# Tokens of a selective scan by VectorE block transpositions and SBUF-to-SBUF transfers in place of TensorE transposes

## The reference

```python
zxbcdt = x @ Win                       # per direction; 256 -> 512 (z) + 640 (x, B, C) + 8 (dt)
xBC = silu(causal_conv4(xBC) + convb)  # depthwise, 4 taps
dt = softplus(dt + dtb); dA = exp(dt * A)
h = dA_t * h + dt_t * B_t (x) x_t      # per head: 8 heads of 64, state 64; scan over 512 tokens
y = C_t . h + D * x
y = y * silu(z); y = y * rsqrt(mean(y*y) + 1e-5) * normw
out = y @ Wout                         # reversed direction likewise, on flipped tokens
x = x + concat(out_fwd, out_rev) @ Wo + bo
x = x + layernorm(x) @ W.T + b + (layernorm(x) @ V_r) @ C.T
```

## Time and profile before

| | |
|---|---|
| median of 3 runs | 630.82 us (629.98 to 631.05) |
| span of the profiled execution | 629.0 us |
| TensorE busy | 592.0 us, 94% |
| ScalarE busy | 547.2 us, 87% |
| VectorE busy | 503.6 us, 80% |
| POOL busy | 409.4 us, 65% |
| granted TensorE clock, mean | 0.995 |

### The profile page before, as it was taken

One profiled execution on the slowest core, in us unless ns is written; L12 is line 12 of the kernel. 1 busy time (PEld: TensorE's weight loads), 2 busy tenths in 40 slices (PEclk: granted clock), 3 DMA queues, 4 the chain that ended last, 5 costly groups with the idle time before them and its releaser, 6 DMA issues.

```text
span 629.0 us, 13895 instructions
## 1 busy us (share of the span) xinstructions
PE 592.0 (94%) x4320; PEld 461.0 (73%) x4320; DVE 503.6 (80%) x991; ACT 547.2 (87%) x1197; POOL 409.4 (65%) x427
## 2 busy tenths in 40 slices
PE   1998999999999999999999999999999999999995
PEld 1776687777877777777877778777777777777784
DVE  2669788996979879797888969798797978879663
ACT  4689998979999899988999799897999989997952
POOL 1006948787486864878476874868648684768843
PEclk9999999999999999999999999999999999999997
DMA  7533514236061541418132360614416170343500
GB/s 220 189 109 115 198 40 124 92 106 203 8 200 27 171 114 41 169 28 255 28 116 95 107 204 0 211 25 160 126 28 182 26 241 12 92 122 99 181 1 33
DMA packets 43545, 70.71 MB, mean 112 GB/s; under 512 B 8000, under 2 KB 30592, under 8 KB 43520
## 3 DMA queue, kind: packets, MB, share of 16 engines
q1 hardware_dynamic: 43520, 70.40, 36.7%
HBM read 59.37 MB, written 4.72 MB: 102 GB/s over the span
## 4 chain that ended last, share of the span: by engine, by line
PE 55%; ACT 18%; DVE 13%; issue 8%; POOL 3%; SPq 1%; DMA 1%; DVEq 0%; ACTq 0%; POOLq 0%
PE mi L621 14%; ACT bs L968 8%; PE pj L487 7%; PE py L580 7%; PE pj L489 6%; PE pj L488 6%; DVE xc L1378 5%; PE mi L687 4%; PE py L598 3%; ACT bs L974 2%; ACT L953 2%; DVE bs L1405 2%; DVE ss L1437 2%; ACT xc L935 1%; DVE xres L1445 1%
## 5 line engine op out<-in xcount | busy, mean ns | idle before, releaser
L1378 DVE SCALAR_TENSOR_TENSOR xc<-pj,cw,xc 128x510 f32<-128x510 f32 (+2 forms) x240 | 175.4, 744 | 24.9 <-ACT xc L935 23.0
L968 ACT ACTIVATE bs<-bs,s_all 128x128 f32<-128x128 f32 x512 | 158.4, 388 | 0.2
L1892 POOL TENSOR_TENSOR yg<-yg,sz 128x512 f32<-128x512 f32 x60 | 76.9, 1287 | 81.6 <-DVE yg L1424 81.6
L487 PE MATMUL pj<-xnt_hi,w_hi 128*128 128x512 f32 x288 | 126.1, 438 | 0.9 <-DVE xc L1378 0.8
L489 PE MATMUL pj<-xnt_hi,w_lo 128*128 128x512 f32 x288 | 114.2, 396 | 0.0
L488 PE MATMUL pj<-xnt_lo,w_hi 128*128 128x512 f32 x288 | 113.8, 395 | 0.0
L621 PE MATMUL mi<-wc,yg 128*128 128x256 f32 x480 | 112.1, 386 | 0.8 <-DVE xres L1445 0.2
L621 PEld LDWEIGHTS mi<-wc,yg 128*128 128x128 f32 x480 | 88.6, 190 | 16.9 <-issue 3.3
L1405 DVE TENSOR_TENSOR bs<-bs,gm 128x512 f32<-128x512 f32 x128 | 86.1, 680 | 8.5 <-ACT bs L974 7.7
L1871 POOL TENSOR_TENSOR xw<-xdt,w_end 128x512 f32<-128x512 f32 x48 | 49.6, 1045 | 49.8 <-ACT w_end L953 40.9
L1390 DVE TENSOR_TENSOR xdt<-mi,dt 128x512 f32<-128x512 f32 x64 | 42.8, 688 | 44.6 <-PE mi L547 44.2
(11 more groups left out here) (149 smaller groups left out, 1021.6 us busy)
## 6 DMA issues: line engine op xcount, KB each, us to landing
bs<-rows_dram SPq DMA_DIRECT2D x64, 512.0 KB, 5.4
es<-rows_dram SPq DMA_DIRECT2D x128, 96.0 KB, 3.0
xres<-in_x SPq DMA_DIRECT2D x8, 512.0 KB, 3.6
cc<-bcm SPq DMA_DIRECT2D x32, 128.0 KB, 2.3
out<-ot SPq DMA_DIRECT2D x32, 128.0 KB, 3.4
xin<-in_x SPq DMA_DIRECT2D x7, 512.0 KB, 5.3
rows_dram<-s_rows SPq DMA_DIRECT2D x128, 4.0 KB
cz<-bcm SPq DMA_DIRECT2D x16, 128.0 KB, 2.4
```

Source lines behind the costliest of these rows:

```text
L487: pe.matmul(ps[:], hi(k), xnt_hi[:, k, :], start=(k == 0), stop=False)
L968: i = nc.scalar.activation(bs[:, h, Q * c:Q * c + Q], bs[:, h, Q * c:Q * c + Q], ACT.Relu, bias=s_all[:, d, 0, c, h:h + 1], scale=-1.0)
L1378: i = dve.scalar_tensor_tensor(xc[:, t, to], pj[bank][:, of], cw[:, d, t, KW - 1 - s:KW - s], xc[:, t, to], ALU.mult, ALU.add)
L1892: pool.tensor_tensor(yg[:, d, p, :], yg[:, d, p, :], sz[:, d, p, :], ALU.mult).then_inc(yg_ready, 1)
```

## The change

TensorE transposes neither x nor B any more. `turn` (VectorE) transposes each of the five tiles of a unit, four of `xs` and the one of `bcm`, in blocks of 32x32. Its output goes into `turned`, in which the five tiles lie interleaved: one tile's elements are five words (20 bytes) apart. This puts the tokens in the right order within each block of 32 partitions. `carry` (SP) then moves the blocks to their partitions, with 16 SBUF-to-SBUF transfers per unit, each from 32 partitions to 32 partitions in runs of 640 bytes (80 KB), into `tok`. `step` (VectorE) multiplies the x part of `tok` with dt in place, four times per unit. `state` and `intra` read their weights, and `decayed_x` its input, from `tok`, at every fifth word. `xw` now lies in the same bytes as `turned`. The copies of B (ScalarE) and 5 of the 19 uses of the `mi` banks per unit go. `decayed_c` now waits for C's copies itself. All engines' lists of calls, and SP's, are put in new orders, the opening's loads too.

```diff
+SQ = 32
+BLK = P // SQ
...
-        xdt = sb("xdt", [P, NC, DI])
-        xw = sb("xw", [P, NC - 1, DI])
-        btok = sb("btok", [P, NC, NS])
+        turned = sb("turned", [P, BLK, NC, SQ * (1 + KI)])
+        xw = turned[:].rearrange("p b c r -> p (b c r)")[:, 0:(NC - 1) * DI].rearrange("p (j n) -> p j n", j=NC - 1)
+        tok = sb("tok", [P, NC, P, 1 + KI])
...
+            def carry(b, d):
+                sp.wait_ge(turn_ready, (1 + KI) * (2 * b + d + 1))
+                alone(sp)
+                pair_done(b, d, KI - 1)
+                for i in range(BLK):
+                    for q in range(BLK):
+                        sp.dma_start(tok[SQ * q:SQ * q + SQ, :, SQ * i:SQ * i + SQ, :].rearrange("p c r t -> p c (r t)"),
+                                     turned[SQ * i:SQ * i + SQ, q]).then_inc(tok_loaded[i], 16)
...
-            def b_tokens(phase, it, b, d):
...
-            def x_tokens(phase, it, b, d, j):
...
-                                   btok[:, ORDER[d][j], :], heads[:, :, MEMBERS[half], :], start=True, stop=True, skip_group_check=True)
+                                   tok[:, ORDER[d][j], 0:NS, KI], heads[:, :, MEMBERS[half], :], start=True, stop=True, skip_group_check=True)
...
+                if p == 0:
+                    pe.wait_ge(step_ready, NC * (u + 1))
...
-                        pe.matmul(py[bank][HP * half:HP * half + HP, Q * c:Q * c + Q], xdt[:, c, HP * h:HP * h + HP],
+                        pe.matmul(py[bank][HP * half:HP * half + HP, Q * c:Q * c + Q], tok[:, c, HP * half:HP * half + HP, p],
...
+            def turn(b, d, t):
+
+                u = 2 * b + d
+                if t < KI:
+                    dve.wait_ge(xs_ready, KI * u + t + 1)
+                else:
+                    dve.wait_ge(bc_ready, u + 1)
+                dve.transpose(turned[:].rearrange("p b c (r t) -> p c b r t", t=1 + KI)[:, :, :, :, t],
+                              xs[:, d, t, :] if t < KI else bcm[:, d, :]).then_inc(turn_ready, 1)
+
+            def step(b, d, j):
+
+                if j == 0:
+                    for i in range(BLK):
+                        dve.wait_ge(tok_loaded[i], 16 * BLK * (2 * b + d + 1))
+                    dve.wait_ge(dt_ready[d], b + 1)
                 c = ORDER[d][j]
...
+                own = tok[:, c, :, 0:KI].rearrange("p (z q) t -> p z t q", z=2)
+                i = dve.tensor_tensor(own, own, dt[:, d, c, :].rearrange("p (t z) -> p z t", z=2).unsqueeze(3).broadcast_to([P, 2, KI, HP]),
+                                        ALU.mult)
+                i.then_inc(step_ready, 1)
...
+                pool.wait_ge(step_ready, NC * (2 * b + d) + j + 1)
...
+                if p == 0:
+                    pool.wait_ge(cc_loaded[d], 48 * (b + 1))
```

More of the change, by code:

```diff
@@ L1556, in reversed_scan @@
+                outputs(b, 1, 1)
+                weights(phase, it, b, 1, 7)
+                conv(nxt, 0, 2, 3)
                 conv(nxt, 0, 4, 1)
+                turn(nxt, 0, 4)
+                conv(nxt, 0, 3, 3)
                 conv(nxt, 0, 4, 2)
-                conv(nxt, 0, 3, 3)
+                turn(nxt, 0, 0)
                 conv(nxt, 0, 4, 3)
+                turn(nxt, 0, 1)
+                turn(nxt, 0, 2)
+                turn(nxt, 0, 3)
+                s_rest(phase, it, 0)
                 outputs(b, 1, 2)
@@ L1612, in first_scan @@
+                turn(b, 1, 4)
+                weights(phase, it, b, 0, 7)
+                turn(b, 1, 0)
+                turn(b, 1, 1)
+                s_rest(phase, it, 1)
+                turn(b, 1, 2)
+                turn(b, 1, 3)
                 outputs(b, 0, 2)
@@ L1710, in forward_scan @@
-                conv(b, 1, 1, 3)
-                norm2_bn(phase, it, last, 1)
+                turn(b, 1, 4)
+                s_copy(phase, it, 1)
+                conv(b, 1, 2, 2)
+                norm2_aggr(last, 0)
+                norm2_aggr(last, 1)
+                outputs(b, 0, 0)
+                conv(b, 1, 2, 3)
+                weights(phase, it, b, 0, 5)
                 mix(phase, it, last, 1, 2)
```

762 lines of the change are left out of this document (358 added, 404 removed).

## The result

The changed kernel takes 753.64 us (751.9 to 756.03) beside 630.4 us (629.89 to 631.05) for the kernel before on the same chip: 1.196 times the time, interval 1.193 to 1.199. I had forecast 680 us and a range of 617 to 730. The direction was right; the measured time lies outside the range, 74 us above the forecast. The profiled execution spans 752.0 us, 123.0 more than the 629.0 before.

The account below looks back on a forecast made before the run. TensorE, busy 72.0 of 73.6 us a turn, bounds the kernel; the change moves the bound to VectorE. Its 77.4 busy plus 2.6 uncovered carry make 80.0; seven turns add 45 us, the ends 4: forecast 680 us, range 617 to 730.

Parts of the forecast that it names:

- TensorE, minus 5.8 us: TensorE, per turn: transposes of x and B go, 4.6 + 1.2 = 5.8 us, leaving it busy 66.2.
- VectorE, 77.4 us: VectorE's busy time per turn: 56.7 kept, 8.8 for ten `turn`, 11.9 for eight `step` with their waits.
- rival (B): VectorE: gaps cost nothing, `turn` and `step` 0.61 us each, turn 70.2 to 73.1, whole 620 us; 23%.
- The wait for POOL: VectorE's `step`, both inputs in SBUF, waits for POOL: bounds 0 and 1.04 us, taken as 0.35 each.
- The carry, 8.1 us by 355 ns an issue: SP's 16 transfers per direction, priced like `bs`; 2.6 us per turn uncovered by VectorE's work.
- rival (C): SP's carry: 590 ns per issue, 11.8 us per carry, 10.0 uncovered, turn 87.4, whole 732 us; 18%.
- Queued behind the carry at nothing: SP's `es` and `bs` stand 5.7 us later behind `carry`; costed at nothing, up to 5.7 per direction if cover fails.
- rival (D): TensorE: interleaved weights load at half speed, VectorE cheap as in rival (B), turn 74.8, whole 643 us; 7%.
- New orders at nothing: TensorE, ScalarE and POOL: new orders move no new work in and stay 10 us under VectorE; cost nothing.
- The ends, plus 4: Both ends of the run: a carry with little ahead of it, less transposes; bounds 0 and 16, taken as 4 us.

Follow-up runs that it names:

- run 13: Changed kernel without carry transfers, tokens in unbroken runs, each product replaced by a block transposition; 626.96 us, ratio to the kernel before 0.994.
- run 12: Kernel before without TensorE's token transposes and ScalarE's copies of B, buffer filled once, products replaced by block transpositions; 629.07 us, ratio 0.999.
- run 1: Changed kernel without the carry's transfers and the steps' wait for them, tokens' tile filled once; 680.74 us, ratio to the kernel before 1.080.
- run 14: Kernel before kept whole, only the product reads its own buffer in SBUF in place of PSUM; 657.07 us, ratio 1.044.
- Run 2: Changed kernel, each carry's bytes in four transfers of 128 partitions in place of sixteen of 32, moves between bands left out; 682.5 us.
- run 4: Changed kernel with only SP's forward order changed: the last two `bs` transfers go ahead of the forward carry; 752.54 us.
- run 3: Changed kernel with SP's order changed: `bs` transfers ahead of the forward carry and all four output stores ahead of the reversed one; 766.19 us.
- runs 10: Changed kernel's orders with no token work but the products: no block transposes or transfers, buffer filled once and read in unbroken runs; 644.77 us.
- run 11: Kernel before, in its old orders, without TensorE's transposes and ScalarE's copies of B; products read an SBUF buffer filled once; 649.95 us.
- Run 6: Changed kernel without carry transfers and their wait, and with tokens read and written in unbroken runs; 643.9 us, ratio 1.0205.
- run 1 and 5: The second, 5: changed kernel with all token operations in unbroken runs in place of words 20 bytes apart, transfers and orders kept; 711.04 us.

## Why the prediction was wrong in size

The forecast was 80.0 us a turn and 4 at the ends; measured were 87.0 and 29.6. The 7.0 a turn are 6.4 more of waiting for the carry (9.0 for 2.6) and 4.8 of other idle time of VectorE that I had at nothing, less 4.2 of busy time. Seven times 7.0, and 25.6 at the ends, make the 74 us but for rounding. So the steps that failed are the carry's price, the ends, and that VectorE would wait for nothing else. By its own steps:

- **TensorE, minus 5.8 us.** As busy time right: 66.6 us a turn in run 13, for 66.2. As a gain it failed: "TensorE work that goes away can be gained" is false here, since run 12, the kernel before without transposes and products, takes 629 us. A busy share of 98% hid that the transposes lay over waits for POOL, VectorE and ScalarE that end ahead of the states (idle 40.1 us in run 12, 8.0 before). In the changed kernel TensorE is busy 71.0 in place of 66.2; weight loads with gaps were costed at nothing and take 199 in place of 137 ns, and at the granted clock of 0.90 to 0.92 matmuls take longer (L621: 421 ns mean for 386 over the run, 6.20 us for 3.72 where the clock was 0.59).
- **VectorE, 77.4 us.** 73.2 measured. `turn` was set at 0.88, the middle of its bounds, and is 1.14, the upper end. The argument for the middle was empty: the two reductions whose slope was to speak against a price are the two that the price per element had been taken from. For the rest, the ten `turn`s of a turn, partly in a row, take 10.7 us in place of 8.8. `step` with its wait was set at 1.49, and the 16 of two turns take 19.8 us, 1.24 each, 2.0 a turn less. The remaining 4 us are work that got cheaper, 2.5 of them `wd`, which took 1.45 us on average before and 0.18 now, since it no longer falls behind a long POOL operation; rival (B) had named that. The other 1.5 I did not place. The rule of the Trainium skill that I had weighed (Vector Engine (DVE) Microarchitecture Reference, Measured stream behaviour on trn2: 1.98 ns a column where every stream hops at each element, a row for hops of 4 KiB and not of 20 bytes; 1.09 us for a step by my estimate) agrees with the undisturbed step of 1.08; for the `turn`, with an output alone that hops, it gave an estimated 0.95 and the trace shows 1.14.
- **The wait for POOL.** 0.35 us per step was about twice what the changed kernel shows (1.24 on average, 1.08 undisturbed), where the steps come late and POOL stands waiting for them. In run 1, without that lateness, it is 0.41 (1.49 for 1.08). In the kernel before, run 14, it is 0.58 (1.27 for 0.69), and the 27 us that it costs are about its own sum. The Trainium skill, page SBUF — State Buffer, section SBUF: two separate sides, says that VectorE and GpSimd share one pair of ports, which a VectorE operation with two SBUF inputs and a GpSimd operation that reads SBUF hold in turn, the other blocked meanwhile. The traces agree: products of 0.69 us become 1.52, POOL's 1.3 becomes 1.7, and `turn` with its one input keeps to 1103 to 1190 ns beside the same POOL.
- **The carry, 8.1 us by 355 ns an issue.** This is the largest error, 6.4 us a turn and 45 in all. An issue takes 601 ns, 12.1 us from the first to the step, which is rival (C), given 18% and 732 us. Its turn of 87.4 us is nearly the measured 87.0, by some luck: it had 77.4 busy and 10.0 waiting, and 73.2, 9.0 and 4.8 of other idle time came. I had chosen the row with the most rows per transfer in place of the row nearest in kind, `cc` at 590 ns. Run 2 shows that size has almost no say in it (662 ns for four times the bytes).
- **Queued behind the carry at nothing.** The queue stretched further than its 5.7 us: `bs` by up to 8.2 us and the output's stores, which I had not listed at all, with `dt_bias` and TensorE behind them. Sending `bs` first (run 4) gained nothing, so its share beside the tokens' lateness is nil; sending the stores first as well (run 3) lost 13 us, as it delays the carry. `dt_bias` with a buffer of its own was not tried.
- **Interleaved loads, rival (D).** The loads did get slower, but TensorE was no bound, and its busy time fell by only 0.9 us a turn without the gaps. As I read it gaps cost by VectorE and POOL on the chain. Rival (B) fell with the `turn` at 1.14.
- **New orders at nothing.** As a total nearly right, 5 us better than the old ones with the same work (runs 10 and 11), with TensorE's transposes left out in both. By parts not: some 13 us won in the turns, 10 lost at the ends.
- **The ends, plus 4.** They measured 29.6. By the same reckoning run 1 has 52.7 - 7 x 4.7 = 20, so transfers make some 9.5 of it. Run 6 has 12, so gaps make some 8.5. The last 12 stand in runs 10 and 13 too, whatever the token work, and not in runs 11, 12 and 14, so they belong to the new orders, of which the opening's is one.

As a sum from the changed kernel down: transfers 73, gaps 37 (43 if taken first), the product's source 17, and what is left is 3 us under before. The waits of run 1 and 5 overlap by 6, the difference between 753.6 - 73 - 43 and 643.9.

What stays open: how much of the loss TensorE's lower clock makes, since it fell along with the waits and no run changed one without the other. And whether earlier steps, or another opening, would win something was not tried.

## What to carry to other kernels

Before work is moved off the engine that is busy longest, ask what waits end under that work; leave it out in a run that puts made-up values in its place, and see whether the time falls at all. Here it did not (run 12), and that one run would have warned against the change. Mind that nothing else changes with it: run 11 also moved the product's source, and got slower. A transfer cost 0.6 us on its queue here, and hardly more with four times the bytes, so at these sizes count issues, not bytes, and read the issue price from the row nearest in kind. A product whose source moved from PSUM to SBUF began to share with GpSimd; price that in full, even on an engine that is not the fullest. And reckon the ends by themselves: they were a quarter of this loss.

## What was not expected of the hardware

- 80 KB in 32 partitions take 601 ns to issue and 320 KB in 128 partitions 662, and the latter land only 1.5 us later.
- Pieces of 128 bytes in place of 640, five times as many, raised the steps' wait by only 1.25 us for each carry (82.6 - 62.6 over 16), landing 2.7 us in place of 2.2.
- One fp32 product of 512 columns takes 0.69 us out of PSUM, 1.52 (median; mean 1.27) out of SBUF beside POOL, and 1.08 out of SBUF undisturbed when its words lie 20 bytes apart. A block transposition of 512 columns takes 0.70 us into runs and 1.14 into words 20 bytes apart.
- A weight load of 64 columns 20 bytes apart takes 199 ns for 137; GpSimd's product takes 2.0 us for 1.04, and still 1.42 in runs where VectorE's product now works at the same time. Its least is 1.31 with gaps, and it is back at 1.04 on average in run 13, where transpositions take the place of VectorE's products.
- The kernel before with 5.8 us a turn less to do on TensorE is not faster.
